# Two attention layers over tokens: which wait starts the scores, which engine reads the turned rows, and in what order GpSimd adds the mask

## The chip, the cores and the metric

The kernel runs on one core of a Trainium2 chip. The metric is the device time of one execution in microseconds. The kernel before takes 4070.14 us, the median of three runs (4067.51 to 4077.97).

## What is computed

Five blocks follow one another on 8 batches of 256 tokens with 512 features: an attention over the context, an attention over channels, two attentions over tokens (self and cross), an MLP, and a recurrent block. The change is in the two attentions over tokens. Cut to these, the reference is:

```python
def attention(q, k, v, mask):                       # 16 heads of 32
    scores = jnp.einsum('bhqd,bhkd->bhqk', q, k) / jnp.sqrt(jnp.float32(HD))
    scores = scores * mask - 10000.0 * (1.0 - mask)
    probs = jax.nn.softmax(scores, axis=-1)
    return jnp.einsum('bhqk,bhkd->bhqd', probs, v)

ln_out = layernorm(hidden_states, ln1_s, ln1_b)
q, k, v = jnp.split(ln_out @ w_qkv + b_qkv, 3, axis=-1)
x = hidden_states + merge_heads(attention(heads(q), heads(k), heads(v), ltor_mask)) @ w_ao + b_ao
ln_out = layernorm(x, ln2_s, ln2_b)
q, (k, v) = ln_out @ w_q + b_q, jnp.split(encoder_states @ w_kv + b_kv, 2, axis=-1)
x = x + merge_heads(attention(heads(q), heads(k), heads(v), cross_mask)) @ w_co + b_co
```

## The kernel before

`token_attentions` runs both layers as one stream of 16 batches, numbered u or b, with layer 2 directly behind layer 1. Each engine has its own program of the same loop (`each_pass`): batches 0 and 1 of a layer are written out, batches 2 to 5 are a loop of two passes with two batches each, 6 and 7 are written out again. The order of work on an engine is written by hand, and the engines meet only in semaphores. A helper such as `step(g, u, n)` computes the count a semaphore must have reached.

Products that need full accuracy are done in three terms: each operand is held as a rounded part (hi) and a rest (lo), and hi x hi, lo x hi and hi x lo are added in PSUM.

A batch goes through these steps:

- **Rows.** ScalarE normalises x into `xn`. TensorE turns it with 8 transposes into the two PSUM banks of `ps_t` (`turn_rows`, L1190). From there the rows are read twice, each time scaled and shifted by the layernorm's weights: ScalarE writes the rounded rows `lnT_hi` (`round_rows`, L1367), VectorE the plain rows `lnT` (`keep_rows`, L1511). The two go crosswise over the banks: ScalarE bank 0, then 1, VectorE bank 1, then 0, and each waits for the other between. VectorE then makes `lnT_lo` (`split_rows`, L1518). The rows of batch u+2 are made at the end of batch u.
- **Fills.** TensorE makes q, k and v of batch u+1 during batch u in six units, Q0, Q1, K0, K1, V0, V1 (`fill`, L1216 and L1218), all through the one bank `ps_p`. ScalarE reads the Q and K units out (`keep`), VectorE the V units (`keep_values`, L1524). Each fill waits until the one before it has been read. In layer 2, k and v come from the context `cs`, which is loaded, rounded by ScalarE (L1374) and split by GpSimd (`split_context`, L1133).
- **Scores and softmax.** The 16 heads are 4 groups of 4 heads; a group is two steps of 2 heads, so a batch has 8 steps. TensorE computes a group's scores (`scores`, L1228); those of group 0 wait for the V1 unit's read-out. For each step, VectorE multiplies by the mask (`multiply`, L1530), GpSimd adds the mask's sum term (L1156, called mask sum below), VectorE takes the negated maxima (`maxima`, L1538), ScalarE the exponentials (L1400), and TensorE turns the probabilities into `ps_t` (`turn`, L1240), from where VectorE reads the even steps and ScalarE the odd ones (`keep_turn`, L1543 and L1407) into `pT`.
- **Mix.** TensorE mixes a group's values (`mix`, L1250) and spreads the inverted masses (L1254). VectorE multiplies the two (`keep_mix`, L1554 and L1556), ScalarE rounds (L1380), GpSimd splits (`split_mix`, L1137), and TensorE applies the output weights (`project_out`, L1270).

The last steps of batch u (turns 6 and 7, mix 3) and its output run inside batch u+1. At a boundary TensorE's order is: V1 fill of u+1, rows of u+2, mix 2 of u, scores 0 of u+1, turn 6 of u, Q0 fill of u+2, turn 7 of u. Between the steps GpSimd also has `root` (L1128, for the layernorm of u+2; VectorE's `make_offset`, L1499, waits for it and stands between the maxima of steps 2 and 3) and `add_bias` (L1143, x plus the output bias of u+1). SP issues all transfers in one queue; its load of x for batch u+2 (L1052) waits for `add_bias` of batch u, and the loads of context and mask and the store stand behind it. Some batches also round and split a weight of the next layer (L1359, L1503).

Of the kernel before, what the change touches and what calls it, by code (L numbers as in the profile page):

```python
# [33 lines left out]
def at(g, per_pass, k, unit=1):  # L34

    return (g * per_pass + k + 1) * unit
# [880 lines left out]
def token_attentions(nc, semaphores, layers):  # L920
# [11 lines left out]
    with ExitStack() as ctx:  # L932
# [53 lines left out]
        c_loaded, c_rounded, c_split = (sem("c_" + n) for n in ("loaded", "rounded", "split"))  # L986
        ln_turned, ln_rounded, ln_full, ln_split = sem("ln_turned", 1), sem("ln_rounded", 2), sem("ln_full", 2), sem("ln_split", 1)
        stored = sem("stored", 16)
# [129 lines left out]
        def _(pool):  # L1118
# [32 lines left out]
            def batch(g, u, near):  # L1151
                pool.wait_ge(mask_split, at(g, 2, u))
                for n in range(STEPS):
                    tile = pr[n % RING][:, :, :, :].rearrange("p h t k -> p h (t k)")
                    pool.wait_ge(masked_mul, step(g, u, n))
                    pool.tensor_tensor(tile, tile, ma[u][:, :, :].rearrange("p t k -> p (t k)").unsqueeze(1).to_broadcast([P, 2, TT * TOK]),  # L1156
                                       ALU.add).then_inc(masked, 1)
                    if n == 0 and near.prev is not None:
                        split_mix(g, u - 1, 2)
                    if n == 1 and near.next is not None and layers[near.next].cT is not None:  # L1160
                        split_context(g, u + 1)
                    if n == 2:
                        if near.after is not None:
                            root(g, u + 2)
                        if near.prev is not None:
                            split_mix(g, u - 1, 3)
                    if n == 4:
                        split_mix(g, u, 0)
                    if n == 6:
                        split_mix(g, u, 1)  # L1170
                        if near.next is not None:
                            add_bias(g, u + 1, near.next)
# [8 lines left out]
        def _(pe):  # L1181
            pe.wait_ge(ident_made, 2)

            def turn_rows(g, b):
                pe.wait_ge(normalised, at(g, 2, b))
                pe.wait_ge(turned_kept, step(g, b - 2, 5))
                pe.wait_ge(ln_full, at(g, 4, 2 * b - 1))
                for f in range(FT):
                    for m in range(TT):
                        mm = pe.transpose(ps_t[:, f // 2, f % 2, m * P:(m + 1) * P], xn[:, m, f * P:(f + 1) * P], ident[:, :])  # L1190
                mm.then_inc(ln_turned, 1)

            def fill(g, b, unit, i):
# [6 lines left out]
                if encoder:  # L1200
                    pe.wait_ge(c_rounded, context_at(g, b))
                    terms = ((w_hi[n], cs_hi), (w_lo[n], cs_hi), (w_hi[n], cs_lo))
                else:
                    pe.wait_ge(ln_rounded, at(g, 4, 2 * b + 1))
                    terms = ((w_hi[n], lnT_hi), (w_lo[n], lnT_hi), (w_hi[n], lnT_lo))
# [15 lines left out]
            def scores(g, u, k):  # L1221
                if k == 0:
                    pe.wait_ge(fill_kept, unit_at(g, u, "V1"))
                pe.wait_ge(masked_mul, step(g, u, 2 * k - 1))
                for m in range(TT):
                    for h in range(GROUP):
                        r = slice(h * DH, (h + 1) * DH)
                        mm = pe.matmul(ps_s[:, h, m, :], qT[u][r, k, m * P:(m + 1) * P], kT[u][r, k, :], start=True, stop=True)  # L1228
                mm.then_inc(scored, 1)

            def turn(g, u, n, rows_turned=True):
                pe.wait_ge(exped, step(g, u, n))
                pe.wait_ge(turned_kept, step(g, u, n - 1))
                if n == STEPS - 2 and rows_turned:
                    pe.wait_ge(ln_rounded, at(g, 4, 2 * (u + 2) + 1))
                    pe.wait_ge(ln_full, at(g, 4, 2 * (u + 2) + 1))
                for i in range(2):
# [5 lines left out]
            def mix(g, u, k):  # L1243
                pe.wait_ge(turned_kept, step(g, u, 2 * k + 1))
                pe.wait_ge(inverted, group(g, u, k))
                pe.wait_ge(mixed_kept, group(g, u, k - 1))
# [85 lines left out]
        def _(act):  # L1332
# [28 lines left out]
            def round_rows(g, b, i):  # L1361
                act.wait_ge(ln_turned, at(g, 2, b))
                for bank in range(2):
                    if bank == 1:
                        act.wait_ge(ln_full, at(g, 4, 2 * b))
                    for f in (2 * bank, 2 * bank + 1):
                        ins = act.activation(lnT_hi[:, f, :], ps_t[:, bank, f % 2, :], ACT.Identity, bias=ln_sb[i][:, 1, f:f + 1],  # L1367
                                             scale=ln_sb[i][:, 0, f:f + 1])
                    ins.then_inc(ln_rounded, 1)

# [109 lines left out]
        def _(dve):  # L1480
# [23 lines left out]

            def keep_rows(g, b, i):
                dve.wait_ge(ln_turned, at(g, 2, b))
                for bank in (1, 0):
                    if bank == 0:
                        dve.wait_ge(ln_rounded, at(g, 4, 2 * b))
                    for f in (2 * bank, 2 * bank + 1):  # L1510
                        ins = dve.tensor_scalar(lnT[:, f, :], ps_t[:, bank, f % 2, :], ln_sb[i][:, 0, f:f + 1], ln_sb[i][:, 1, f:f + 1],  # L1511
                                                ALU.mult, ALU.add)
                    ins.then_inc(ln_full, 1)

            def split_rows(g, b):
                dve.wait_ge(ln_full, at(g, 4, 2 * b + 1))
                dve.wait_ge(ln_rounded, at(g, 4, 2 * b + 1))
                dve.tensor_tensor(lnT_lo[:, :, :], lnT[:, :, :], lnT_hi[:, :, :].bitcast(F32), ALU.subtract).then_inc(ln_split, 1)  # L1518
# [44 lines left out]
            def before():  # L1563
                statistics(1, 0)
                make_offset(1, 0)
                keep_rows(1, 0, 0)
                split_weight("Q", 0)
                split_rows(1, 0)
                statistics(1, 1)
                make_offset(1, 1)  # L1570
                split_weight("K", 0)
                split_weight("V", 0)
                keep_values(1, 0, 0, 0)
                keep_values(1, 0, 1, 0)
                keep_rows(1, 1, 0)
                split_rows(1, 1)

            def batch(g, u, near):
                dve.wait_ge(mask_loaded[u], arrived(g, u))
                multiply(g, u, 0)  # L1580
# [52 lines left out]
                if near.next is not None:  # L1633
                    keep_values(g, u + 1, 1, near.next)
                if near.after is not None:
                    keep_rows(g, u + 2, near.after)
                keep_mix(g, u, 2)
                if near.after is not None:
                    split_rows(g, u + 2)

# [1177 lines left out]
```

## Time and profile before

| | |
|---|---|
| median of 3 runs | 4070.14 us (4067.51 to 4077.97) |
| profiled execution: its time / its span | 4071.54 us / 4069.7 us |
| TensorE busy, share of the span | 3572.6 us, 88% |
| VectorE busy | 2260.3 us, 56% |
| GpSimd busy | 1998.3 us, 49% |
| ScalarE busy | 1821.8 us, 45% |
| mean granted TensorE clock | 0.947 |
| the two token attentions | from about 1750 to 2541 us |

Busy shares are means over five blocks. What the change is worth is read from the stretch between 1750 and 2541 us: there, from the waits of each engine and from the order of instructions around the end of a batch. Since the engines' programs are fixed lists, an instruction that waits holds all behind it on its engine.

### The profile page before, as it was taken

How to read it: one execution, taken by the hardware profiler on the slowest of the kernel's cores; microseconds unless marked ns; L12 is line 12 of the kernel's file. 1: busy time of each engine (PE TensorE's matmuls, PEld its weight loads, DVE VectorE, ACT ScalarE, POOL GpSimd, SP SyncE). 2: the span in 40 equal slices, each digit the busy share in tenths (PEclk: the TensorE clock that was granted, in tenths of full speed). 3: DMA queues.
4: the chain of work that ended last, by engine and by line, in shares of the span. 5: the costliest groups of instructions: out<-in, count | busy, mean ns of one | idle time of the engine just before them, and what ended most of it. 6: DMA issues, size and time to landing. Idle time of an engine off the chain costs nothing. (4 is left out here: it accounts for less than half of the span.)

```text
span 4069.7 us, 64007 instructions
## 1 busy us (share of the span) xinstructions
PE 3572.6 (88%) x23616; PEld 2696.4 (66%) x23616; DVE 2260.3 (56%) x2778; ACT 1821.8 (45%) x4207; POOL 1998.3 (49%) x1015
## 2 busy tenths in 40 slices
PE   8969999999999999859989997699967888888876
PEld 5757676777777677547777775588845555555543
DVE  2435454444444444447777766555427777767772
ACT  1135454555555455556666665444422332323321
POOL 1145555555555555335555554355525555555552
PEclk9989999999999999989999999799979999998988
DMA  4231111111111111020021110300030000000000
GB/s 134 67 127 58 54 58 54 68 43 58 53 59 58 54 58 53 21 96 27 26 68 48 43 39 23 106 21 21 16 129 6 12 17 17 17 7 12 12 11 16
DMA packets 107558, 189.87 MB, mean 47 GB/s; under 512 B 13344, under 2 KB 32032, under 8 KB 105632
## 3 DMA queue, kind: packets, MB, share of 16 engines
q1 hardware_dynamic: 105120, 181.97, 13.1%
q8 instruction: 191, 3.13, 0.3%
q10 hardware_dynamic: 2176, 4.19, 0.3%
q14 instruction: 71, 0.58, 0.0%
HBM read 160.97 MB, written 25.17 MB: 46 GB/s over the span
## 5 line engine op out<-in xcount | busy, mean ns | idle before, releaser
L780 POOL TENSOR_TENSOR l_pr<-l_pr,l_inv 128x1024 f32<-128x1024 f32 x256 | 485.9, 1919 | 429.7 <-DVE l_inv L824 429.7
L690 ACT ACTIVATE l_pr<-l_ps_s,l_top 128x512 f32<-128x512 f32 x512 | 348.1, 691 | 385.3 <-DVE l_top L820 385.3
L1156 POOL TENSOR_TENSOR tok_pr<-tok_pr,tok_ma 128x1024 f32<-128x1024 f32 x128 | 308.0, 2407 | 309.2 <-DVE tok_pr L1530 295.2
L2288 POOL TENSOR_TENSOR rec_rs<-rec_sE,rec_rT 128x1024 f32<-128x1024 f32 x128 | 321.8, 2515 | 248.3 <-DVE rec_sE L2675 246.2
L775 POOL TENSOR_TENSOR l_x_lo<-l_zu,l_x_hi 128x2048 fp32r<-128x2048 f32 x64 | 289.5, 4523 | 274.0 <-ACT l_x_hi L674 274.0
L820 DVE TENSOR_REDUCE l_top<-l_ps_s 128x2 f32<-128x1024 f32 x256 | 301.3, 1216 | 57.8 <-PE l_ps_s L557 57.8
L565 PEld LDWEIGHTS l_ps_t<-l_ident,l_pr 128*128 128x128 f32 x2048 | 227.8, 142 | 104.5 <-issue 103.0
L2675 DVE TENSOR_TENSOR_SCAN rec_sE<-rec_wE,rec_ps_v 128x1024 f32<-128x1024 f32 x128 | 292.7, 2286 | 4.9
L557 PE MATMUL l_ps_s<-l_k,l_q 64*128 64x512 f32 x1024 | 264.6, 637 | 29.8 <-issue 29.8
L565 PE MATMUL l_ps_t<-l_ident,l_pr 128*128 128x128 f32 x2048 | 275.3, 278 | 3.6 <-ACT l_pT L695 3.6
L1400 ACT ACTIVATE tok_pr<-tok_pr,tok_shift 128x256 f32<-128x256 f32 x512 | 253.8, 499 | 27.6 <-DVE tok_shift L1538 27.3
L836 DVE TENSOR_TENSOR l_o_lo<-l_ps_a,l_o_hi 128x512 fp32r<-128x512 f32 x64 | 44.2, 691 | 381.3 <-ACT l_o_hi L700 381.3
L547 PE MATMUL l_ps_b<-l_wv,l_zu 128*128 128x128 f32 x2048 | 239.4, 275 | 0.0
L1538 DVE TENSOR_REDUCE tok_shift<-tok_pr 128x4 f32<-128x1024 f32 x128 | 155.7, 1217 | 149.6 <-POOL tok_pr L1156 147.9
L577 PE MATMUL l_ps_a<-l_pT,l_v 128*64 128x512 f32 x1024 | 235.5, 602 | 1.8 <-ACT l_pT L695 1.8
L547 PEld LDWEIGHTS l_ps_b<-l_wv,l_zu 128*128 128x128 f32 x2048 | 234.0, 192 | 0.0
L828 DVE COPY l_pT<-l_ps_t 128x512 f32<-128x512 f32 x256 | 175.4, 685 | 70.7 <-PE l_ps_t L565 70.2
L557 PEld LDWEIGHTS l_ps_s<-l_k,l_q 64*128 64x128 f32 x1024 | 91.2, 192 | 167.8 <-issue 167.3
L695 ACT ACTIVATE l_pT<-l_ps_t 128x512 f32<-128x512 f32 x256 | 152.4, 595 | 70.4 <-PE l_ps_t L565 70.4
L524 PE MATMUL l_ps_a<-l_x_hi,l_w_lo 128*128 128x256 f32 x512 | 151.7, 296 | 32.2 <-POOL l_x_lo L775 32.2
L1240 PE MATMUL tok_ps_t<-tok_ident,tok_pr 128*128 128x128 f32 x1024 | 143.1, 285 | 32.0 <-DVE tok_pT L1543 13.0
L1787 POOL TENSOR_TENSOR mlp_cube<-mlp_cube,mlp_pre 128x512 f32<-128x512 f32 x64 | 89.6, 1400 | 163.8 <-DVE mlp_cube L1950 163.8
(357 smaller groups left out, 9385.1 us busy)
## 6 DMA issues: line engine op xcount, KB each, us to landing
l_zu<-x SPq DMA_DIRECT2D x64, 512.0 KB, 3.7
l_zu<-in_c SPq DMA_DIRECT2D x64, 512.0 KB, 4.6
l_w_raw<-in_L_w_qk SPq DMA_DIRECT2D x8, 1024.0 KB, 7.6
tok_xs<-x SPq DMA_DIRECT2D x16, 512.0 KB, 3.7
x<-tok_xb SPq DMA_DIRECT2D x16, 512.0 KB, 2.8
l_xt<-in_xT SPq DMA_DIRECT2D x8, 512.0 KB, 6.5
l_ct<-in_cT SPq DMA_DIRECT2D x8, 512.0 KB, 7.8
l_xn<-in_x SPq DMA_DIRECT2D x8, 512.0 KB, 4.7
```

Source lines behind the costliest of these rows:

```text
L547: mm = pe.matmul(ps_b[:, t * P:(t + 1) * P], zu[b % 2][:, s, t * P:(t + 1) * P], wv[:, t // 2 * SLOTS + s, :], start=(s == 0), stop=(s == ...
L557: pe.matmul(ps_s[:, t % 2, h, :], q[b % 2][own(h), t * P:(t + 1) * P], k[b % 2][own(h), :], start=True, stop=True).then_inc(scored, 1)
L565: mm = pe.transpose(ps_t[h][:, m, :], pr[t][:, h, m * P:(m + 1) * P], ident[:, :])
L577: mm = pe.matmul(ps_a[own(h), :], v[b % 2][:, t, own(h)], pT[h][:, t, :], start=(t == 0), stop=(t == QT - 1), skip_group_check=True)
L690: act.activation(pr[t][:, h, :], ps_s[:, t % 2, h, :], ACT.Exp, bias=top[:, t, h:h + 1], accum_out=mass[:, t, h:h + 1]).then_inc(exped, 1)
L775: pool.tensor_tensor(x_lo[b % 2][:, :, :], zu[b % 2][:, :, :], x_hi[b % 2][:, :, :].bitcast(F32), ALU.subtract).then_inc(x_split, 1)
L780: pool.tensor_tensor(pr[t][:, :, :], pr[t][:, :, :], inv[:, t, :].unsqueeze(2).to_broadcast([P, 2, FEAT]), ALU.mult).then_inc(scaled, 1)
L820: dve.tensor_reduce(top[:, t, :], ps_s[:, t % 2, :, :], AXIS.X, ALU.max, negate=True).then_inc(topped, 1)
L1156: pool.tensor_tensor(tile, tile, ma[u][:, :, :].rearrange("p t k -> p (t k)").unsqueeze(1).to_broadcast([P, 2, TT * TOK]), ALU.add).then_i ...
L1400: ins = act.activation(tile, tile, ACT.Exp, bias=shift[n % RING][:, i, m:m + 1], accum_out=mass[n // 2 % 2][:, m, n % 2 * 2 + i:n % 2 * 2 ...
L2288: pool.tensor_tensor(rs[j % 2][:, :, :], sE[j % 2][:, :, :], rT[s][:, :, :], ALU.mult).then_inc(rs_made, 1)
L2675: dve.tensor_tensor_scan(sE[j % 2][:, :, :].rearrange("p c t -> p (c t)"), wE[s][:, :, :].rearrange("p c t -> p (c t)"), ps_v[j % 2][:, :, ...
```

## The change

The change has four parts, all inside `token_attentions`:

1. The scores of group 0 wait for the read-out of K1, no longer of V1. `mix` of group 0 waits for V1 in their place.
2. `keep_rows` on VectorE goes. ScalarE's `round_rows` reads all four feature blocks from both banks into the plain `lnT`, then makes `lnT_hi` by one Copy of 128x1024 from SBUF. TensorE's next users of `ps_t` wait for the read-out alone (`ln_full`), the fills for the Copy (`ln_rounded`).
3. VectorE's `split_rows` stands at the head of the next batch instead of at the end of this one; between the two places there is nothing on that engine.
4. GpSimd does mask sums 2k and 2k+1 one after the other, and the side work (`split_mix`, `split_context`, `root`, `add_bias`) after the odd one.

```diff
@@ gpsimd, batch, after the mask sum of step n
-                    if n == 0 and near.prev is not None:
-                        split_mix(g, u - 1, 2)
-                    if n == 1 and near.next is not None and layers[near.next].cT is not None:
-                        split_context(g, u + 1)
-                    if n == 2:
+                    if n == 1:
+                        if near.prev is not None:
+                            split_mix(g, u - 1, 2)
+                        if near.next is not None and layers[near.next].cT is not None:
+                            split_context(g, u + 1)
+                    elif n == 3:
                         if near.after is not None:
                             root(g, u + 2)
                         if near.prev is not None:
                             split_mix(g, u - 1, 3)
-                    if n == 4:
+                    elif n == 5:
                         split_mix(g, u, 0)
-                    if n == 6:
+                    elif n == 7:
                         split_mix(g, u, 1)
                         if near.next is not None:
                             add_bias(g, u + 1, near.next)
@@ tensor
             def turn_rows(g, b):
-                pe.wait_ge(ln_full, at(g, 4, 2 * b - 1))
+                pe.wait_ge(ln_full, at(g, 2, b - 1))
             def fill(g, b, unit, i):
-                    pe.wait_ge(ln_rounded, at(g, 4, 2 * b + 1))
+                    pe.wait_ge(ln_rounded, at(g, 2, b))
             def scores(g, u, k):
                 if k == 0:
-                    pe.wait_ge(fill_kept, unit_at(g, u, "V1"))
+                    pe.wait_ge(fill_kept, unit_at(g, u, "K1"))
             def turn(g, u, n, rows_turned=True):
                 if n == STEPS - 2 and rows_turned:
-                    pe.wait_ge(ln_rounded, at(g, 4, 2 * (u + 2) + 1))
-                    pe.wait_ge(ln_full, at(g, 4, 2 * (u + 2) + 1))
+                    pe.wait_ge(ln_full, at(g, 2, u + 2))
             def mix(g, u, k):
                 pe.wait_ge(turned_kept, step(g, u, 2 * k + 1))
+                if k == 0:
+                    pe.wait_ge(fill_kept, unit_at(g, u, "V1"))
@@ scalar
             def round_rows(g, b, i):
                 act.wait_ge(ln_turned, at(g, 2, b))
-                for bank in range(2):
-                    if bank == 1:
-                        act.wait_ge(ln_full, at(g, 4, 2 * b))
-                    for f in (2 * bank, 2 * bank + 1):
-                        ins = act.activation(lnT_hi[:, f, :], ps_t[:, bank, f % 2, :], ACT.Identity, bias=ln_sb[i][:, 1, f:f + 1],
-                                             scale=ln_sb[i][:, 0, f:f + 1])
-                    ins.then_inc(ln_rounded, 1)
+                act.wait_ge(ln_split, at(g, 2, b - 1))
+                for f in range(FT):
+                    ins = act.activation(lnT[:, f, :], ps_t[:, f // 2, f % 2, :], ACT.Identity, bias=ln_sb[i][:, 1, f:f + 1],
+                                         scale=ln_sb[i][:, 0, f:f + 1])
+                ins.then_inc(ln_full, 1)
+                act.wait_ge(ln_full, at(g, 2, b))
+                act.activation(lnT_hi[:, :, :], lnT[:, :, :], ACT.Copy).then_inc(ln_rounded, 1)
@@ vector
-            def keep_rows(g, b, i):
-                dve.wait_ge(ln_turned, at(g, 2, b))
-                for bank in (1, 0):
-                    if bank == 0:
-                        dve.wait_ge(ln_rounded, at(g, 4, 2 * b))
-                    for f in (2 * bank, 2 * bank + 1):
-                        ins = dve.tensor_scalar(lnT[:, f, :], ps_t[:, bank, f % 2, :], ln_sb[i][:, 0, f:f + 1], ln_sb[i][:, 1, f:f + 1],
-                                                ALU.mult, ALU.add)
-                    ins.then_inc(ln_full, 1)
-
             def split_rows(g, b):
-                dve.wait_ge(ln_full, at(g, 4, 2 * b + 1))
-                dve.wait_ge(ln_rounded, at(g, 4, 2 * b + 1))
+                dve.wait_ge(ln_rounded, at(g, 2, b))
             def batch(g, u, near):
+                if near.prev is not None and near.next is not None:
+                    split_rows(g, u + 1)
                 dve.wait_ge(mask_loaded[u], arrived(g, u))
                 multiply(g, u, 0)
...
                 if near.next is not None:
                     keep_values(g, u + 1, 1, near.next)
-                if near.after is not None:
-                    keep_rows(g, u + 2, near.after)
                 keep_mix(g, u, 2)
-                if near.after is not None:
-                    split_rows(g, u + 2)
```

The two calls of `keep_rows` in VectorE's `before()` go as well, and the semaphores `ln_full` and `ln_rounded` count once a batch instead of twice.

## Rows read from the trace of the kernel before

**Rows 1.** The page's first line: the span.

```profile
span 4069.7 us, 64007 instructions
```

**Rows 2.** Windows: busy us (instructions) of each engine, clock, DMA share, GB/s.

```profile
1790.00:2540.00 750.00, 676.76 (x6392) 551.54 (x6392) 555.90 (x752) 468.58 (x1387) 414.94 (x229) 0.97 0.11 38
```

**Rows 3.** Waits from 1790 to 2540 us: total us, times, the longest.

```profile
ACT tok_lnT_hi L1367 <- DVE tok_lnT L1511: 37.0, 14, 4.9
...
PE tok_ps_s L1228 <- DVE tok_v L1524: 21.3, 14, 3.6
...
PE tok_ps_t L1240 <- DVE tok_pT L1543: 13.0, 17, 2.9
...
PE tok_ps_t L1240 <- ACT tok_lnT_hi L1367: 9.9, 12, 1.0
```

**Rows 4.** Timeline of a plain boundary: start us, us, instruction [idle before it <- releaser].

```profile
1919.49 0.39 SPq L1052 DMA_DIRECT2D tok_xs<-x  x1
...
1921.03 1.02 ACT L1367 ACTIVATE tok_lnT_hi<-tok_ps_t,tok_ln_cols 128x256 fp32r<-128x256 f32 x2 [0.79 <-PE tok_ps_t L1190]
...
1921.69 1.22 DVE L1538 TENSOR_REDUCE tok_shift<-tok_pr 128x4 f32<-128x1024 f32 x1 [3.57 <-POOL tok_pr L1156]
...
1922.83 0.68 DVE L1524 TENSOR_TENSOR tok_v<-tok_ps_p,tok_rows 128x512 f32<-128x512 f32 x1
...
1923.64 1.15 PE L1228 MATMUL tok_ps_s<-tok_kT,tok_qT 32*128 32x256 f32 x16 [1.22 <-DVE tok_v L1524]
...
1925.24 0.41 DVE L1554 COPY tok_share<-tok_ps_o 128x256 f32<-128x256 f32 x1
...
1925.52 1.09 PE L1240 MATMUL tok_ps_t<-tok_ident,tok_pr 128*128 128x128 f32 x8 [0.73 <-ACT tok_lnT_hi L1367]
1925.69 0.42 DVE L1556 TENSOR_TENSOR tok_cx<-tok_ps_o,tok_share 128x256 f32<-128x256 f32 x1
...
1926.03 1.21 DVE L1518 TENSOR_TENSOR tok_lnT_lo<-tok_lnT,tok_lnT_hi 128x1024 fp32r<-128x1024 f32 x1
...
1929.65 1.07 PE L1240 MATMUL tok_ps_t<-tok_ident,tok_pr 128*128 128x128 f32 x8 [0.19 <-DVE tok_pT L1543]
...
1935.08 1.28 DVE L1486 BATCH_NORM_STATS2 tok_stats<-tok_xs 128x6 f32<-128x512 f32 x2
```

**Rows 5.** Groups by line, 1790 to 2540 us: busy us, mean ns | idle before.

```profile
L1137 POOL TENSOR_TENSOR tok_cx_lo<-tok_cx,tok_cx_hi 128x256 fp32r<-128x256 f32 x64 | 46.9, 733 | 14.1 <-ACT tok_cx_hi L1380 14.1
...
L1367 ACT ACTIVATE tok_lnT_hi<-tok_ps_t,tok_ln_cols 128x256 fp32r<-128x256 f32 x60 | 30.6, 559 | 52.8 <-DVE tok_lnT L1511 37.0 <-PE tok_ps_t L1190 15.8
L1511 DVE TENSOR_SCALAR tok_lnT<-tok_ps_t,tok_ln_cols 128x256 f32<-128x256 f32 x60 | 28.5, 536 | 0.2 <-PE tok_ps_t L1190 0.2
...
L1374 ACT ACTIVATE tok_cs_hi<-tok_cs 128x1024 fp32r<-128x1024 f32 x8 | 8.4, 1053 | 0.0
```

**Rows 6.** L1499 by its line (ns min/median/max), and the timeline at 1767 us.

```profile
L1499 DVE SCALAR_TENSOR_TENSOR tok_offset<-tok_moments,tok_rstd x16: 160/208/2317, 1755.9 to 2416.2; 128x2 f32<-128x2 f32 x16
...
1767.69 2.37 POOL L1143 TENSOR_TENSOR tok_xb<-tok_xs,tok_rows 128x1024 f32<-128x1024 f32 x1
1767.76 2.32 DVE L1499 SCALAR_TENSOR_TENSOR tok_offset<-tok_moments,tok_rstd 128x2 f32<-128x2 f32 x1 [0.81 <-POOL tok_rstd L1128]
```

**Rows 7.** Timeline: boundaries at 1826, at 2204, and the loop edge at 2344.

```profile
1826.60 2.38 POOL L1156 TENSOR_TENSOR tok_pr<-tok_pr,tok_ma 128x1024 f32<-128x1024 f32 x1
...
1830.15 2.28 DVE L1503 TENSOR_TENSOR tok_w_loO<-tok_wsK,tok_w_hiO 128x2048 fp32r<-128x2048 f32 x1
...
1840.69 1.03 PE L1240 MATMUL tok_ps_t<-tok_ident,tok_pr 128*128 128x128 f32 x8
...
2203.56 1.00 ACT L1367 ACTIVATE tok_lnT_hi<-tok_ps_t,tok_ln_cols 128x256 fp32r<-128x256 f32 x2
...
2215.18 1.03 PE L1240 MATMUL tok_ps_t<-tok_ident,tok_pr 128*128 128x128 f32 x8
...
2348.64 2.09 PE L1228 MATMUL tok_ps_s<-tok_kT,tok_qT 32*128 32x256 f32 x16 [4.39 <-issue]
```

More of the change, by code:

```diff
@@ L986, in token_attentions @@
         c_loaded, c_rounded, c_split = (sem("c_" + n) for n in ("loaded", "rounded", "split"))
-        ln_turned, ln_rounded, ln_full, ln_split = sem("ln_turned", 1), sem("ln_rounded", 2), sem("ln_full", 2), sem("ln_split", 1)
+        ln_turned, ln_full, ln_rounded, ln_split = (sem(n, 1) for n in ("ln_turned", "ln_full", "ln_rounded", "ln_split"))
         stored = sem("stored", 16)
@@ L1565, in before @@
                 make_offset(1, 0)
-                keep_rows(1, 0, 0)
                 split_weight("Q", 0)
@@ L1574, in before @@
                 keep_values(1, 0, 1, 0)
-                keep_rows(1, 1, 0)
                 split_rows(1, 1)
             def batch(g, u, near):
+                if near.prev is not None and near.next is not None:
+                    split_rows(g, u + 1)
                 dve.wait_ge(mask_loaded[u], arrived(g, u))
```

## The prediction, made before the changed kernel was run

> **What bounds the kernel now.** The page first: its span is 4069.7 us [rows 1], the profiled execution took 4071.54 us and the median of the timed runs is 4070.14 us. My sum is made against 4071.54 and moved down by the 1.4 us between them at the end. The windows view then shows how the stage of the change (1790 to 2540 us, sixteen batches of two attention layers) is limited [rows 2]: TensorE is busy 677 of 750 us, VectorE 556, ScalarE 469, GpSimd 415, at a granted clock of 0.97. So the change can win only what TensorE stands still, 73 us, and at the most what it touches of these. The view of waits names them [rows 3]: 21.3 us in 14 waits before the first scores of a batch (for VectorE's `tok_v`), 9.9 us in 12 before the transposes that reuse `ps_t` (for ScalarE's `tok_lnT_hi`), 13.0 us in 17 for VectorE's `tok_pT`. ScalarE in turn waits 37.0 us in 14 for VectorE's part of the row read-out. Fourteen is the number of batch boundaries: the stall is at one place, once a batch.
>
> The timeline of one boundary shows how it hangs together [rows 4]. TensorE turns the rows of a later batch, mixes group 2, and stands still 1.22 us until 1923.64, since VectorE reads the values (V1) only behind the maxima of step 7, and these started at 1921.69 after 3.57 us of waiting for GpSimd's mask sum. The scores run, and TensorE waits 0.73 us more: the two banks of `ps_t` are read twice, ScalarE and VectorE crosswise, ScalarE's first half from 1921.03 and its last until 1925.5. Then come split_rows at 1926.03, multiply 0, keep_turn 6, and with 0.19 us of wait TensorE's turn of step 7 at 1929.65. Idle at this boundary: 1.22 + 0.73 + 0.19 = 2.14 us.
>
> **The change, part by part.**
>
> *Scores wait for K1 alone.* K1 is kept long before the boundary, so the 1.22 us wait goes. The V1 wait stands now before mix 0, half a period later, and at the fill of Q0 (every fill waits for the one before), so V1 must still be read by then. Scores start at 1923.64 - 1.22 = 1922.42, turn 6 can follow 1.15 us later.
>
> *ScalarE alone reads the turned rows.* Gone are four VectorE reads of 0.536 us; ScalarE's four of 0.559 us stay, now into the plain tile, and a Copy of 128x1024 from SBUF is new. That Copy has a twin in the trace, the rounding of the context at 1.053 us [rows 5]. ScalarE's first two take 1.02 us together [rows 4], so four end 2.04 us after 1921.03, at 1923.07: `ps_t` is free 2.4 us earlier, before turn 6 wants it, and the 0.73 us go too. The Copy ends at about 1924.2 (2.04 + 1.05 + two handovers of under 0.1 us: 3.17 us after the first read). ScalarE ends there 1.3 us earlier than now (1925.5), though it works 1.05 us more (14 times, 15 us of its 469), so the exponentials of step 7 queued behind are not late.
>
> *What is late next.* VectorE's split_rows needs the Copy; it is only written down at the head of the next batch and has the same place in the queue. With its read work gone VectorE is free before 1924.2, so split_rows starts at 1924.2 in place of 1926.03, and all queued behind it (multiply 0, keep_turn 6, TensorE's turn of step 7) moves by the same 1.83 us, to 1927.8. TensorE itself would be ready 2.14 - 0.19 = 1.95 us earlier, so VectorE's chain ends last and sets the gain: 1.83 us. Bounds from rows: not under 0.8 us if the Copy took twice its row, and not over 2.14 us, TensorE's whole idle time there.
>
> *GpSimd's order.* Mask sum 7 comes before split_mix 1 (0.73 us) and the bias sum (2.4 us), so the maxima of step 7 and V1 no longer wait 3 us. In plain boundaries V1 then waits for its fill alone, and the gain is that already counted. Mask sum 1 passes one split_mix, mask sum 3 another and root. The context split stays behind mask sum 1 and waits for ScalarE there anyway; its PE readers see no change. Root is queued after mask sum 3 (2.4 us a sum), and VectorE's make_offset, which stands before the maxima of step 3, waits for it: with split_mix 3 right behind it the maxima start about 0.2 us later than now instead of 1.4 us earlier. Cover: TensorE has a whole project_out between these and the turn that reads them. Without cover, 14 x 0.2 = 3 us of loss. On SP's queue the load of x waits for the bias sum, now 2.4 us later, with context, mask and store behind it. It was issued at 1919.49 and is read by VectorE's statistics at 1935.08 [rows 4], so 15 us cover a delay of 2.4. Hidden.
>
> *A lock between GpSimd and VectorE.* A tiny VectorE instruction (make_offset, usually 0.2 us) took 2.32 us at 1767.76 while the bias sum ran from 1767.69 to 1770.06 [rows 6]. The moved bias sum now runs where batch 1's split of the O weight stands: mask sum 7 would start 3.05 us earlier than its 1826.60 [rows 7], the bias sum would run from 1826.7 to 1829.1, and the split (2.28 us), ready at 1827.2, would start at 1829.1. The Trainium skill, page "SBUF — State Buffer", section "SBUF: two separate sides", says the same of a VectorE instruction with two SBUF inputs against a GpSimd one that reads SBUF: the later fully blocks. By that the sum loses these 1.9 us; without it batch 1 would gain 6.2 us instead of 4.3. It speaks against moving the bias sum, and the row agrees with it.
>
> **The sum.** Fifteen boundaries. Eleven plain: 11 x 1.83 = 20.1 us. Batch 1: split 1829.1 to 1831.4, V1 and the two steps of keep_mix 1.5 us (0.68 + 0.41 + 0.42) [rows 4], split_rows at 1832.8, and 3.62 us (1929.65 - 1926.03) to the turn: 1836.4, against 1840.69 [rows 7]: 4.3 us. The first of layer 2 with a weight split, at 2204: reads start at 2203.56, so the turn comes at 2203.56 + 3.17 + 3.62 = 2210.35 against 2215.18: 4.8 us. The last, with no row read-out: at least the scores' wait of a plain one, 1.2 us. The loop edge at 2344 waits 4.39 us for issue, not for a semaphore [rows 7]: 0.3 us. Together 30.7 us. For small waits on `tok_pT` inside the periods and the last batch, where GpSimd's order counts since no fills cover it, between 0 and 6 us (14 x 0.2 us at turn 7 stay, and half of the other ten could go); I take 3, the middle, because no row is nearer to one end. At the stage's start the first Copy delays one fill by 1 us and the missing VectorE reads bring the first weight split 1 us forward: 0. Sum 33.7 us, rounded 34: 4071.5 - 34 = 4037.5, less 1.4: **4036 us**.
>
> **Rivals.**
> 1. *Half is given back.* VectorE's chain moves by only about 1.0 us a boundary, since ScalarE begins to read later (its exponentials of step 6 depend on a GpSimd that is pushed elsewhere) or handovers cost more. For it: ScalarE waited only 0.79 us before 1921.03. Against: nothing in steps 5 and 6 is moved later. The plain ones give 11 us, the others two thirds of their 10.6: 18 us, 4052 us. Chance 0.14.
> 2. *More is won.* At half clock the 16 score matmuls take 2.09 us at 2348 and 1.15 us at 1923 [rows 4, 7]. If fewer stalls keep the clock up elsewhere and the loop edge's 4.39 us is not there in a run, 4.4 us and some 5 us of half clock come on top: 4026 us. Chance 0.15.
> 3. *Nothing comes of it.* make_offset and the splits meet GpSimd's sums as at 1767.76 in every batch, 2.1 us each, and nothing covers it: 14 x 2.1 = 29 us back, 4065 us. For it: the row. Against: only split_mix 3 (0.73 us) stands behind root. Chance 0.05.
> 4. *Slower.* One engine now does rows and rounding in series, and the exponentials of step 6 stand before them. The gain is used up if the first read starts 1.83 us later than now, and the kernel is slower by over 12 us (0.9 us in each of 14) if it starts 2.7 us later: exponentials of step 6 that end after 1923.7 in that boundary, where they ended before 1920.3. At 3.2 us it would give 4070 + 14 x 1.37 = 4089 us. Against: that would need mask sum 6 to be late, which the change does not touch. Chance 0.04.
>
> My forecast, 4026 to 4046 by itself, has the remaining 0.62. The range to 8 in 10 takes in rival 2 in part and rival 1: 4024 to 4054 us. A difference under 0.3% (12 us) is about what a measurement of this kernel can't tell from none. Faster by more: 0.62 + 0.14 + 0.15 = 0.91; within: 0.05; slower: 0.04.
>
> **What would show it.** The wait of the scores for `tok_v` is gone and that of the turns for ScalarE's read too; `tok_pT` holds turn 7 by a few tenths; the period of a plain batch is 1.8 us shorter; ScalarE's Copy takes 1.05 us and its wait for VectorE (37.0 us) is zero; split_rows starts as the Copy ends; VectorE's split of the O weight in batch 1 starts as the bias sum ends. It is wrong if TensorE waits as long for `tok_pT` as it did for the other two, if the maxima of step 3 hold up turn 3, or if issue gaps like that at 2344 come at more boundaries: each costs 4.39 us and some us of half clock after it, so three would undo a third of the gain.

## The result and the profile after

The changed kernel takes 4028.1 us, the median of four runs (4027.5 to 4029.1); the kernel before took 4071.5 beside it (4067.5 to 4078.0). The ratio is 0.9892, 95% interval 0.9875 to 0.9909: 43 us less, where 34 were forecast. The forecast was 4036 us, in a range of 4024 to 4054.

The page of the changed kernel: the line of [rows 1] and the busy time of each engine.

```profile
span 4026.3 us, 63937 instructions
...
PE 3557.7 (88%) x23616; PEld 2684.2 (67%) x23616; DVE 2252.9 (56%) x2714; ACT 1839.6 (46%) x4223; POOL 1996.3 (50%) x1015
```

From here on "the stage" is the time from the first scores to the first load of the next block, and "the rest" what follows it to the end. The windows view (columns as in [rows 2]) of the stage and the rest, first of the kernel before, then of the changed one:

```profile
1789.86:2545.63 755.77, 676.90 (x6393) 551.68 (x6392) 556.46 (x752) 468.62 (x1387) 415.48 (x232) 0.96 0.12 38
2545.63:4069.70 1524.07, 1242.38 (x6464) 918.29 (x6464) 913.41 (x841) 519.48 (x1132) 745.55 (x423) 0.91 0.08 28
...
1790.39:2509.53 719.14, 668.17 (x6393) 544.77 (x6392) 547.75 (x692) 484.20 (x1402) 412.63 (x232) 0.98 0.12 40
2509.53:4026.30 1516.77, 1234.70 (x6464) 911.79 (x6464) 915.89 (x841) 519.63 (x1132) 746.11 (x423) 0.92 0.08 28
```

The stage was 755.8 us and is 719.1: 36.6 us less. The other 7 us of the 43 lie in the rest, in blocks that no edit touches. The two gains are of different kinds. In the stage TensorE stood still 78.9 us and now 51.0, so 27.9 us are waiting that went. The remaining 8.7 are the same 6393 matmuls in less busy time (676.9 to 668.2 us), at a granted clock of 0.98 in place of 0.96. In the rest TensorE stands still as long as before (281.7 and 282.1 us); its busy time fell by 7.7 us, at a clock of 0.92 in place of 0.91. So about 28 of the 43 us are waiting and 15 are clock.

The waits in the stage of the changed kernel, beside [rows 3]:

```profile
DVE tok_offset L1501 <- POOL tok_rstd L1128: 25.1, 14, 1.8
...
PE tok_ps_t L1240 <- DVE tok_pT L1534: 13.5, 22, 1.6
...
DVE tok_lnT_lo L1509 <- ACT tok_lnT_hi L1371: 11.7, 13, 3.2
```

The 21.3 us before the scores, the 9.9 us for ScalarE's read and ScalarE's own 37.0 us are gone. `tok_pT` still holds TensorE, 0.6 us a time on average, and new waits stand on VectorE: 11.7 us for the Copy, 25.1 us for root.

The timeline of the plain boundary of [rows 4], as it is now:

```profile
1912.27 1.22 DVE L1529 TENSOR_REDUCE tok_shift<-tok_pr 128x4 f32<-128x1024 f32 x1 [0.51 <-POOL tok_pr L1156]
...
1913.80 0.69 DVE L1515 TENSOR_TENSOR tok_v<-tok_ps_p,tok_rows 128x512 f32<-128x512 f32 x1 [0.30 <-PE tok_ps_p L1217]
...
1914.67 1.94 ACT L1367 ACTIVATE tok_lnT<-tok_ps_t,tok_ln_cols 128x256 f32<-128x256 f32 x4 [0.79 <-PE tok_ps_t L1191]
...
1916.00 1.15 PE L1229 MATMUL tok_ps_s<-tok_kT,tok_qT 32*128 32x256 f32 x16
...
1916.64 1.06 ACT L1371 ACTIVATE tok_lnT_hi<-tok_lnT 128x1024 fp32r<-128x1024 f32 x1
...
1917.73 1.23 DVE L1509 TENSOR_TENSOR tok_lnT_lo<-tok_lnT,tok_lnT_hi 128x1024 fp32r<-128x1024 f32 x1 [0.71 <-ACT tok_lnT_hi L1371]
...
1921.37 1.06 PE L1240 MATMUL tok_ps_t<-tok_ident,tok_pr 128*128 128x128 f32 x8 [0.19 <-DVE tok_pT L1534]
```

V1 is read at 1913.80, 2.2 us before the scores, which wait for nothing. split_rows starts as the Copy ends, 3.06 us after the first read (3.17 forecast), and turn 7 follows 3.64 us later (3.62). The idle time at this boundary fell from 2.14 us to 0.19.

### The profile page after: what moved, and what is told of

It reads as the page before. It is cut to its first block and busy times, and to the rows that moved or that the text cites. A ratio compares the mean times of both kernels' runs of the same rounds, so it can differ in the third digit from the quotient of the medians.

```text
span 4026.3 us, 63937 instructions
## 1 busy us (share of the span) xinstructions
PE 3557.7 (88%) x23616; PEld 2684.2 (67%) x23616; DVE 2252.9 (56%) x2714; ACT 1839.6 (46%) x4223; POOL 1996.3 (50%) x1015
## 5 line engine op out<-in xcount | busy, mean ns | idle before, releaser
L1529 DVE TENSOR_REDUCE tok_shift<-tok_pr 128x4 f32<-128x1024 f32 x128 | 155.5, 1216 | 46.9 <-POOL tok_pr L1156 44.2
L1811 PE MATMUL mlp_ps_h<-mlp_ln_hi,mlp_w_lo 128*128 128x256 f32 x512 | 145.3, 284 | 23.1 <-DVE mlp_w_lo L1929 15.1
```

## The experiments

### Each part by itself

The diff of the first: the scores' wait alone, on the kernel before.

```diff
@@ scores, k == 0
-                    pe.wait_ge(fill_kept, unit_at(g, u, "V1"))
+                    pe.wait_ge(fill_kept, unit_at(g, u, "K1"))
@@ mix
+                if k == 0:
+                    pe.wait_ge(fill_kept, unit_at(g, u, "V1"))
```

> The kernel before with one edit: the scores of a batch wait for K1 alone, and the wait for V1 stands before mix 0. Theory of the chain (the idle times at a boundary are not added; turn 6 waits for ScalarE's last read at 1925.5 and turn 7 for VectorE's split_rows at 1926.03, and neither moves): the 21.3 us of waits for tok_v go and come back as waits for ScalarE's read of the rows, about as many; time 1 to 3 us less than before, near 4069 us, most of it at the last boundary, which has no row read-out. Rival (idle times are additive): 14 x 1.22 = 17 us and more, 18 to 21 us less, near 4051 us, and the wait of the turns for ScalarE's read stays at 9.9 us.

Measured: 4072.2 us against 4069.9, ratio 1.0001 (0.9992 to 1.001); stage 757.3 us. The wait of [rows 3] for `tok_v` is gone and stands elsewhere. Its waits over the same stretch have this line:

```profile
PE tok_ps_t L1240 <- ACT tok_lnT_hi L1369: 31.2, 13, 4.7
```

That wait was 9.9 us before: 21.3 more, the same as vanished. Idle times one behind the other are not a sum of gains; the last of the chain decides.

The second takes the read-out by ScalarE alone (`round_rows`, `split_rows` and their semaphores as in the change) on the kernel before, with the old scores' wait and the old GpSimd order.

> The kernel before with one edit: ScalarE alone reads the turned rows and rounds them with a Copy; the scores still wait for V1 and GpSimd has its old order. Theory of the chain: the scores start at 1923.64 as before, turn 6 follows at 1924.8 without its 0.73 us wait, turn 7 about 0.9 us earlier than 1929.65: 14 x 0.9 = 13 us less, near 4058 us; waits for tok_v stay at about 21 us. Rival (this part alone carries the gain, since VectorE's split_rows moves 1.83 us earlier): 28 us or more, under 4043 us.

Measured: 4048.6 us, ratio 0.9944 (0.9930 to 0.9957), stage 739.5 us: 21 us less, between theory and rival (the stage 16 us). The period of a plain batch of layer 1, from one turning of rows to the next, fell from 44.4 to 43.4 us: 1.0, where 0.9 was expected. Layer 2 and a shorter rest, below, gave more.

The third is GpSimd's order alone, the diff of the change in GpSimd's `batch` and nothing else (part 4 of the change; the expectations below call it the third part).

> The kernel before with one edit: GpSimd takes both mask sums of a period first, splits, bias sum and root behind them. Theory of the chain: mask sum 7 and with it VectorE's maxima of step 7 and V1 come 3 us earlier, VectorE is then free when the rows are turned, both halves of the crosswise read-out overlap and end near 1923.15, split_rows near 1924.0: about 2.0 us a boundary and most of batch 1, 33 to 40 us less in all, 4031 to 4038 us, as much as the whole change. ScalarE's wait for VectorE's part of the read-out falls from 37.0 us to under 10. Rival (as my prediction had it, the order counts only for small waits): about 3 us less, near 4068 us.

Measured: 4038.3 us, ratio 0.9921 (0.9907 to 0.9934), stage 720.0 us in a trace of one of its faster runs (4034.8 us). Three quarters of the gain, from the part for which the prediction had put down 3 us. Its plain boundary in the timeline:

```profile
1914.78 1.22 DVE L1539 TENSOR_REDUCE tok_shift<-tok_pr 128x4 f32<-128x1024 f32 x1 [0.51 <-POOL tok_pr L1156]
...
1917.18 2.05 DVE L1512 TENSOR_SCALAR tok_lnT<-tok_ps_t,tok_ln_cols 128x256 f32<-128x256 f32 x4 [0.18 <-PE tok_ps_t L1191]
...
1919.93 1.22 DVE L1519 TENSOR_TENSOR tok_lnT_lo<-tok_lnT,tok_lnT_hi 128x1024 fp32r<-128x1024 f32 x1
```

VectorE waits 0.51 us for mask sum 7 where it waited 3.57 [rows 4]. It has then read V1 and is free when the rows are turned, so that it and ScalarE read their banks at the same time: all is read 2.05 us after the first read, in place of 4.5 (1921.03 to 1925.5). The crosswise read-out was slow because VectorE came late to it. The three stalls of [rows 3] (21.3, 37.0 and 9.9 us) had one main cause, mask sum 7 behind split_mix 1 and the bias sum: ScalarE's wait for VectorE's part fell from 37.0 to 4.7 us, the scores' wait for V1 from 21.3 to 2.8, that of the turns for the read-out from 9.9 to 2.0, and TensorE's turn 7 at 1923.56 waits for nothing. TensorE stands still 55.3 us in the stage.

The fourth is the changed kernel without GpSimd's order.

> The changed kernel with GpSimd's old order (the first two parts together). Theory of the chain: VectorE's maxima of step 7 and V1 still wait for mask sum 7, multiply 0 and keep_turn 6 stand behind them, turn 7 comes about 1.7 us earlier than 1929.65 in each of 14: 24 to 28 us less than before, 4044 to 4048 us. Rival (the third part counts for 3 us only): 40 us less, near 4031 us. If the tail behind the stage (MLP and recurrent part, no edit there) is again 1517 us long and not 1524 as before, the shorter tail goes with something else than the stage's end; if it is either, with the moment at which the stage ends.

Measured: 4041.8 us, ratio 0.9927 (0.9913 to 0.9941), stage 731.5 us: near the theory of the chain, 2 us under its range, and far from the rival. The plain period is 42.6 us: 1.8 less than 44.4, the 1.83 of the prediction. The rest took 1521.0 us, neither the 1524 of the kernel before nor the 1517 of the changed one.

### Which of the four swaps, and what is left for the other parts

```diff
@@ GpSimd's batch, kernel before
-                    if n == 6:
+                    if n == 7:
                         split_mix(g, u, 1)
                         if near.next is not None:
                             add_bias(g, u + 1, near.next)
```

> The kernel before with one edit, a quarter of the third part: only mask sum 7 goes ahead of split_mix 1 and the bias sum; the other three periods keep GpSimd's old order. Theory (the whole worth of the third part is the maxima of step 7 and V1, which start 3 us earlier and leave VectorE free when the rows are turned): 28 to 32 us less than before, near 4040 us, plain periods of 42.2 to 42.4 us in place of 44.4. Rival (all four swaps carry a share, each by its split of 0.7 us): a quarter to a half of the 31.6 us of the run with the whole third part, 8 to 16 us less, near 4058 us.

Measured: 4043.8 us, ratio 0.9927 (0.9913 to 0.9940), stage 724.8 us, plain periods of 42.1 to 42.3 us. This one line is worth 29 us by the medians, 31 in the stage (a trace of its fastest run, 4035.9 us). The other three swaps add nothing to plain periods. In layer 2 half the batches are 0.4 to 1.4 us shorter with them in the trace of the whole order.

> The kernel before with the third and the first part: GpSimd's order, and scores that wait for K1 alone; the rows are still read crosswise. Theory: TensorE has no idle time left at a plain boundary once the order is changed, so only batch 1 gains (its scores waited 2.33 us for V1) and comes back in part as a wait for the read-out: the stage from the first scores to the first load of the next stage takes 717 to 720 us against 720.0 with the order alone and 719.1 with all three; time within 0.3% of the changed kernel. Rival (reading by ScalarE alone is still worth something behind the other two): stage over 724 us.

Measured: 4039.3 us, ratio 0.9915 (0.9901 to 0.9928), stage 724.0 us: it decides for neither. The scores' edit brought nothing that shows behind the order: in batch 1 the 2.33 us before the scores are a wait of 3.44 us for ScalarE's read, now before turn 6, and the loop edge took 52.7 us in place of 51.0.

### The chain behind the Copy

```diff
-                act.activation(lnT_hi[:, :, :], lnT[:, :, :], ACT.Copy).then_inc(ln_rounded, 1)
+                act.activation(lnT_hi[:, :, :], lnT[:, :, :], ACT.Copy).then_inc(ln_first, 1)
+                act.wait_ge(ln_first, at(g, 2, b))
+                act.activation(lnT_hi[:, :, :], lnT[:, :, :], ACT.Copy).then_inc(ln_rounded, 1)
```

> The changed kernel with ScalarE's Copy of the rows done twice (the second one releases split_rows). Theory of the prediction (VectorE's chain behind the Copy sets turn 7, which waited 0.19 us for it at a plain boundary): each of 14 boundaries 1.05 to 1.1 us longer, 15 to 17 us more than the changed kernel with the stage's start, near 4044 us. Rival (TensorE itself is the bound there and the chain has slack): 0 to 4 us more, near 4030 us.

Measured: 4048.6 us (runs near 4040 and near 4049), ratio 0.9936 (0.9922 to 0.9950), stage 733.3 us in a trace of 4040.5 us, 14.2 more than 719.1; plain periods 43.4 to 43.5 us against 42.3 to 42.4. A microsecond more on the Copy is a microsecond more in each period: the chain from ScalarE's read over the Copy and VectorE to turn 7 ends last in the changed kernel, as the prediction had it.

### A version that beats both

```diff
@@ SyncE's batch, changed kernel: at its head
+                if near.after is not None and near.after != near.next:
+                    load_weight("Q", near.after)
+                    load_weight("K", near.after)
+                if near.prev is not None and near.prev != near.cur:
+                    load_weight("O", near.cur)
@@ further down
-                    load_weight("Q", near.after)
-                    load_weight("K", near.after)
...
-                if near.prev is not None and near.prev != near.cur:
-                    load_weight("O", near.cur)
```

> The changed kernel with SyncE issuing the loads of layer 2's weights at the head of their batch, ahead of x, context, mask and store. In the changed kernel ScalarE waits 7.4 us for the Q weight and 4.3 us for the O weight, and TensorE 5.15 us for the exponentials behind the first. Theory: that one idle time goes, the one for O was covered: 5 us less than the changed kernel, stage 714 us, near 4023 us. Rival (the load of x, now behind two weights in the queue, is late for VectorE's statistics and gives it back): within 1 us of the changed kernel or slower.

Measured: 4018.2 us, ratio 0.9865 (0.9850 to 0.9880), stage 711.9 us: 7.3 us shorter, not 5. The batch of the Q weight takes 42.3 us like a plain one, in place of 49.6. The timeline and the windows view of the changed kernel show where the other 2 us were:

```profile
2084.39 1.97 PE L1240 MATMUL tok_ps_t<-tok_ident,tok_pr 128*128 128x128 f32 x8 [5.15 <-ACT tok_pr L1402]
2086.02 2.05 PE L1217 MATMUL tok_ps_p<-tok_w_hiV,tok_lnT_hi 128*128 128x512 f32 x4
...
2084.00:2088.00 4.00, 3.61 (x13) 3.22 (x14) 3.63 (x5) 2.25 (x7) 3.06 (x2) 0.50 0.00 0
```

Behind the 5.15 us in which TensorE stood still the same eight transposes took 1.97 us instead of the 1.09 of turn 6 at 1917.08, and four matmuls 2.05 instead of the 1.19 at 1910.70. The granted clock was 0.50 there, 1.2 GHz. In this batch 5.15 of the 7.3 us were waiting and 2.2 TensorE's busy time (44.2 to 42.0 us). This stall cost its length and then the slower matmuls behind it.

```diff
@@ GpSimd's batch, changed kernel
+                    elif n == 2:
+                        if near.after is not None:
+                            root(g, u + 2)
                     elif n == 3:
-                        if near.after is not None:
-                            root(g, u + 2)
```

> The changed kernel with root back where it was, behind mask sum 2 and ahead of mask sum 3. VectorE's make_offset waited 25.1 us in 14 for it in the changed kernel. Theory (that wait lies ahead of maxima that have a project_out of cover on TensorE): the 25.1 us go, the stage from the first scores to the next stage's first load stays within 1 us of 719.1, time within 0.1% of the changed kernel. Rival (the wait holds up the maxima of step 3 and with them turn 3): 1.8 us in each of 14, stage 694 to 705 us, time under 4015 us.

Measured: 4025.8 us, ratio 0.9887 (0.9870 to 0.9903), stage 719.5 us. The stage is as long, as the theory had it, but the test frees less than it set out to. VectorE's 25.1 us of waiting are gone; `make_offset` itself, now beside a mask sum, takes 1.87 us (median) in place of 0.68. From the maxima of step 2 to those of step 3 it is 1.8 us in place of 2.4 (1891.06 to 1892.86, and 1891.30 to 1893.72). The 0.6 us gained are followed by 0.60 us in which VectorE waits for TensorE's mix. So these 0.6 us a batch cost nothing; the rest of the wait was not removed by this run.

```diff
@@ VectorE's batch, on top of the weight loads
-                if near.after is not None:
-                    statistics(g, u + 2)
...
                 invert(g, u, 0)
+                if near.after is not None:
+                    statistics(g, u + 2)
                 maxima(g, u, 2)
```

> The changed kernel with the weight loads at the head of their batch (as in the run before) and VectorE's row statistics moved from between maxima 1 and keep_mix to behind invert 0. In the changed kernel a 128x2 instruction of the statistics took 2.32 us at 2152.60 while GpSimd's split of the context ran from 2152.52 to 2154.90, and turn 1 then waited 1.07 us for keep_turn 0. Theory: statistics and context split no longer meet, those gaps of 1.0 to 1.4 us go in the batches of layer 2, stage 3 to 5 us shorter than the 711.9 of the run with the loads alone. Rival (the two microseconds of statistics now hold up maxima 2 and turn 2, in every batch): 0 to 14 us longer.

Measured: 4013.7 us, ratio 0.9857 (0.9841 to 0.9874), stage 709.4 us: 2.4 us shorter than with the loads alone, short of 3 to 5. All of it is waiting: TensorE stands still 44.0 us in place of 46.6. The gaps of 1.05 to 1.41 us before turn 1 in layer 2 are gone (`tok_pT` holds TensorE 9.3 us in 17, not 14.2 in 22); waits for exponentials rose from 0.9 to 3.2 us. By the median this is the fastest version, 14 us under the changed kernel; the intervals of the two ratios (0.9841 to 0.9874, 0.9850 to 0.9880) overlap, so that it beats the loads alone is read from the trace and not from the times.

### The part of the gain outside the stage

> The run with GpSimd's order alone once more, unchanged, beside the changed kernel on the same chip. In the traces the two differ by 0.9 us in the stage (720.0 and 719.1 us) but by 10 us in the medians (4038.3 and 4028.1); the rest of the program, which no edit touches, took 3313 us in the one and 3307 in the other. Theory (the rest has two levels some 8 us apart, and chance put the runs on different ones): medians within 5 us of each other, and runs of both kernels on both levels. Rival (the kernel with the crosswise read-out has the longer rest for a reason of its own): again 8 to 12 us apart, the rest 5 us or more longer.

> The changed kernel once more, unchanged. Theory of two levels: some of its runs lie near 4036 us, the others near 4028. Rival: all of them between 4024 and 4031 us, 8 to 12 us under the kernel with GpSimd's order alone.

Measured: 4040.7 us (4038.5 to 4044.4) with the order alone, ratio 0.9923 (0.9909 to 0.9937), and 4028.2 (4026.6 to 4028.5) for the changed kernel, ratio 0.9890 (0.9875 to 0.9905). Again 12.6 us apart, no shared level: the rival holds. The stages were 726.1 and 722.4 us, so a stage's length comes back only within 3 to 6 us, and differences as small as that between single traces (720.0 and 724.0) say nothing. What does not come back is the clock. With the order alone TensorE's busy time in the stage was 664.7 us and now 671.9, and it stood still 55.3 and 54.2; in the changed kernel it stood still 51.0 and 52.3. By this steadier measure ScalarE's read-out, with the scores' edit, is worth 2 to 4 us of waiting in the stage behind the order.

The rest took 1520.8 and 1513.2 us. TensorE stood still 281.4 and 281.2 us of it, so here too the difference, 7.4 us of 7.6, is busy time. The waits of the recurrent block show a difference between the kernels, first in the kernel before, from 2545.63 us on:

```profile
PE rec_ps_v L2407 <- DVE rec_sE L2675: 42.2, 13, 6.4
...
DVE rec_ps_v L2672 <- issue: 5.3, 2, 2.8
```

and in the changed kernel, from 2509.53 us on, where the second line has no counterpart:

```profile
PE rec_ps_v L2394 <- DVE rec_sE L2662: 37.0, 11, 6.4
```

Twice, at 3406.97 and at 3655.92 us, VectorE of the kernel before stood 2.8 and 2.6 us without waiting for any engine, and TensorE waited 5.2 us more for its scan. The stall of 5.2 to 5.5 us is in all six traces of kernels that read the rows crosswise (before, three single edits of them, the pair, and the repeat) and in none of the eight where ScalarE reads alone; the rest of the first took 1520.8 to 1524.1 us, mean 1522.0, that of the others 1513.2 to 1521.0, mean 1517.6.

The stall does not account for the 7 us, though. TensorE stands still in the rest as long before (281.7 us) as after (282.1), so other waits are that much shorter where the stall occurs; over all traces it is 282.0 us on average with the stall and 279.6 without. And three traces without it (ScalarE's rows alone, the changed kernel without the order, the early root) have a rest of 1520.1 to 1521.0 us, at a clock of 0.913 to 0.918, as long as most with it. The time goes mostly with the clock: over the whole run the median granted clock of the timed runs was 0.949 for the order alone, both times, and 0.953 for the changed kernel (0.950 to 0.953 in its eight runs, 0.947 to 0.951 in the forty of the kernel before that stood beside the experiments). So with the order in place the other parts make the kernel 10 to 12.6 us faster by the medians. Of these 2 to 4 are waiting in the stage; in the traces of the repeated pair 8.6 us of 12.5 are TensorE's busy time. Why the clock is higher in the rest of the changed kernel stays open. What makes VectorE's stall is not known either: ScalarE's program and the semaphore counts differ between the two kinds of kernel beside VectorE's, and no run changed one alone.

## Why the prediction was right, point by point

- **The sum as a whole.** The forecast was 34 us, all of it in the stage; the stage gave 36.6. In the two boundaries with a weight split the sum set its new time against the measured old one and so took in 4.5 us of slow clock without naming them (see below); the waiting in it is then 29.5 us, against 27.9 measured. Another 4 us of clock in the stage, and the 7 us in the rest, were in no term. That only 9 us are missing is in part luck: the batches of layer 2 that the sum counted as plain gave 0.8 to 3.3 us in place of 1.83 each, which happens to even out, and of the 15 us that the clock gave the second rival had some 5.
- **The scores' wait and the free `ps_t`.** As forecast: V1 is no longer waited for, and turn 6 waits for ScalarE's read once in the stage, 0.2 us.
- **VectorE's chain sets the gain, 1.83 us a plain boundary.** Without GpSimd's order it was 1.8 us (44.4 to 42.6), with it 2.05 (to 42.3 and 42.4). The chain from ScalarE's first read to turn 7 took 6.70 us, 6.79 by the sum. Doubling the Copy showed that the chain ends last. Eleven by 2.05 would be 22.6 us; but only four boundaries are plain in this sense, and those of layer 2 scatter from 0.3 (the loop edge) to 3.4 us.
- **GpSimd's order, the mis-sized term.** The prediction read "In plain boundaries V1 then waits for its fill alone, and the gain is that already counted" and took 3 us for small waits, 6 at most. On top of the other two parts the order gave 13.7 us by the medians (4041.8 to 4028.1) and 12.4 in the stage: 1.2 in batch 1, 0.2 in a plain batch, 0.6 to 1.6 in most batches of layer 2, 2.6 in the first batch, where the prediction had 0. And alone it gives more than the other two together. As a sum the prediction held, since the parts remove the same waits and cannot be added; as a statement of which part matters it did not. The row was in its hands: 3.57 us of waiting for mask sum 7 [rows 4] is longer than the stall behind it.
- **The lock in batch 1.** Right, and the same lock took a second split. The split of the O weight took 4.01 us in place of 2.28 [rows 7], from 1827.86 us until 2.15 us after the bias sum:

```profile
1827.33 2.39 POOL L1143 TENSOR_TENSOR tok_xb<-tok_xs,tok_rows 128x1024 f32<-128x1024 f32 x1
...
1827.86 4.01 DVE L1505 TENSOR_TENSOR tok_w_loO<-tok_wsK,tok_w_hiO 128x2048 fp32r<-128x2048 f32 x1
```

  The batch gained 4.9 us (48.5 to 43.6), 4.3 forecast. Of the 4.9, 2.6 are waiting and 2.3 busy time: behind a wait of 3.61 us for V1 the 16 score matmuls of the kernel before took 2.09 us, in place of 1.15 in the changed one; the granted clock of the batch was 0.93 and is 1.00.
- **The boundary near 2204.** From ScalarE's first read to turn 7 it was 11.62 us and is 6.89, 4.7 less, where 4.8 was forecast. The sum left out that the weight split is held up here too: it took 4.00 us, at 2181.93, and split_rows started 0.3 us behind the Copy. Over the whole period 3.4 us came (48.1 to 44.6), 2.3 of them clock (0.93 to 1.00). In layer 2 the context split holds VectorE up later in the batch, see below; with the statistics moved away from it this period took 43.8 us.
- **make_offset behind root.** Its wait is 1.8 us in each of 14, more than forecast. The early root took 0.6 us a batch of it away and the stage stayed as long.
- **The end of the stage.** From the last turned rows to the next block 4.3 us less (106.6 to 102.2), all waiting, where 1.2 was the floor and a share of the 3 us came on top: most of the 2.6 us by which the stage beat the sum (36.6 against 34).
- **The rivals.** Half given back: would have needed a late first read; it came 0.79 us after the turn, as before. More won: the time lies nearest to this one, and one half of its reason holds. A higher clock saved 8.7 us of TensorE's busy time in the stage, where the rival had some 5. The other half does not: at the loop edge the gaps of 4.39 and 1.26 us on issue became 2.90 and 2.52 us. Nothing: its lock is there, but cheap. `make_offset` took 0.68 us in place of 0.2 in thirteen batches, a statistics instruction 2.3 us in four, and the second cost about 2.4 us, as its move showed. Slower: no sign.

## What to carry to other kernels

When several engines stall at one place, look for the earliest late instruction and move that first; here one line in GpSimd's order gave 29 us, while removing TensorE's largest wait of [rows 3] by itself gave nothing. Before adding up idle times, ask for each what is late next: 21.3 us of waiting moved on to the next semaphore whole. And split a gain into waiting and busy time, in the untouched blocks too: here a third of it was the same matmuls at a higher granted clock. The waiting came back within 1.3 us between two traces of one kernel, the length of the stage only within 6.

## What was not expected of the hardware

- VectorE can stand 2.6 to 2.8 us on "issue" within a loop, in a block far from the edit. Whether it does goes with which kernel it is: in six traces of six with the crosswise read-out, in none of eight without.
- TensorE's total of waiting behind the stage did not change with this stall; its busy time did, with the granted clock (0.91 and 0.92).
- The lock of [rows 6] also holds an instruction with a single SBUF input, of 128x2, while GpSimd subtracts in SBUF. The Trainium skill, page "SBUF — State Buffer", section "SBUF: two separate sides", names VectorE's two-port modes beside two SBUF inputs as what takes the lock; the trace does not show which mode this one ran in. In the changed kernel:

```profile
2152.52 2.38 POOL L1133 TENSOR_TENSOR tok_cs_lo<-tok_cs,tok_cs_hi 128x1024 fp32r<-128x1024 f32 x1 [2.06 <-ACT tok_cs_hi L1376]
2152.60 2.32 DVE L1497 TENSOR_SCALAR tok_var_eps<-tok_moments 128x2 f32<-128x2 f32 x1
```
